# Sixteen like steps per batch: attention's shifted pass, the output projection and the second feed-forward run on into the next iterations, and the stacked q and k are held once

## The reference

```
x = x + 0.5 * ffn(layernorm(x))
x = x + attention(layernorm(x))      # 16 heads of 16, rope on q and k, softmax, output projection W0
x = x + 0.5 * ffn(layernorm(x))
```

## Time and profile before

| | |
|---|---|
| time, median of 3 runs | 1968.64 us (1968.19 to 1973.37) |
| profiled execution | 1970.23 us |
| its span | 1968.4 us |
| TensorE busy | 1812.3 us, 92% |
| VectorE busy | 1270.6 us, 65% |
| ScalarE busy | 986.5 us, 50% |
| GpSimd busy | 503.9 us, 26% |
| granted TensorE clock, mean | 0.973 of full |

### The profile page before, as it was taken

How to read it: one execution, slowest core, us unless ns; L and a number is a source line. 1 busy time by engine, 2 the same in 40 slices (tenths; PEclk the granted TensorE clock), 3 DMA queues, 4 the chain that set the end, 5 groups by cost and what they waited for, 6 DMA issues and landing times.

```text
span 1968.4 us, 26397 instructions
## 1 busy us (share of the span) xinstructions
PE 1812.3 (92%) x9128; PEld 988.0 (50%) x9128; DVE 1270.6 (65%) x2795; ACT 986.5 (50%) x1954; POOL 503.9 (26%) x663
## 2 busy tenths in 40 slices
PE   6598999999999999999999999999999999998885
PEld 5343545454554645455454545545454554545244
DVE  5476776667666766666676676666667666674631
ACT  1245564545555455555545555564555545454541
POOL 1404132141412214141221414122141412213101
PEclk9698999999999999999999999999999999999897
DMA  4513215060320506032050603206050320505000
GB/s 110 91 17 70 39 28 91 12 108 6 64 51 26 94 12 108 4 71 46 27 93 12 108 4 70 47 21 98 12 108 2 67 52 20 100 1 105 4 12 11
DMA packets 96781, 99.40 MB, mean 50 GB/s; under 512 B 19975, under 2 KB 88328, under 8 KB 96520
## 3 DMA queue, kind: packets, MB, share of 16 engines
q1 hardware_dynamic: 93896, 97.19, 26.7%
q10 hardware_dynamic: 2752, 0.54, 0.2%
HBM read 63.54 MB, written 33.55 MB: 49 GB/s over the span
## 4 chain that ended last, share of the span: by engine, by line
PE 61%; DVE 12%; DMA 12%; ACT 4%; SPq 4%; issue 4%; POOL 2%; POOLq 0%; ACTq 0%; DVEq 0%
PE ps L514 10%; PE ps L502 9%; PE ps L581 8%; PE ps L490 8%; DMA scratch<-parts 7%; DVE mx L832 6%; PE ps L560 6%; SPq L475 4%; PE ps L569 4%; DMA out_dram<-x 4%; PE ps L618 3%; PE ps L636 3%; ACT pr L716 2%; PE ps L621 2%; PE ps L681 2%
## 5 line engine op out<-in xcount | busy, mean ns | idle before, releaser
L832 DVE TENSOR_REDUCE mx<-ps 128x1 f32<-128x512 f32 x1024 | 653.5, 682 | 230.6 <-PE ps L490 229.6
L716 ACT ACTIVATE pr<-ps 128x512 f32<-128x512 f32 x1024 | 555.8, 598 | 292.0 <-PE ps L502 291.5
L490 PE MATMUL ps<-stack 96*128 96x512 bf16 x1024 | 326.1, 387 | 27.1 <-DVE mx L832 23.7
L502 PE MATMUL ps<-stack 98*128 98x512 bf16 x1024 | 323.2, 386 | 20.0 <-ACT pr L716 9.5
L514 PE MATMUL ps<-pr,va 128*32 128x512 f32 x2048 | 274.3, 608 | 4.6 <-ACT pr L716 4.6
L502 PEld LDWEIGHTS ps<-stack 98*128 98x128 bf16 x1024 | 77.5, 100 | 273.5 <-ACT pr L716 174.3
L771 ACT ACTIVATE h<-ps,benc 128x512 f32<-128x512 f32 x128 | 88.0, 687 | 216.2 <-PE ps L560 216.2
L490 PEld LDWEIGHTS ps<-stack 96*128 96x128 bf16 x1024 | 97.8, 98 | 187.8 <-DVE mx L832 91.7
L884 DVE SCALAR_TENSOR_TENSOR ps<-ps,wb,h 128x512 f32<-128x512 f32 x128 | 96.7, 755 | 140.7 <-PE ps L569 140.7
L1029 POOL TENSOR_SCALAR rs<-mv 128x4 f32<-128x4 f32 x48 | 11.6, 242 | 608.3 <-DVE mv L852 602.6
L581 PE MATMUL ps<-xh,w_dh 128*128 128x512 f32 x256 | 124.4, 486 | 9.2 <-DVE ps L884 6.7
(11 more groups left out here) (155 smaller groups left out, 2971.0 us busy)
## 6 DMA issues: line engine op xcount, KB each, us to landing
stack<-scratch SPq DMA_DIRECT2D x384, 128.0 KB, 4.5
scratch<-parts SPq DMA_DIRECT2D x64, 384.0 KB, 5.6
xin<-in_L_attn_x_dram SPq DMA_DIRECT2D x16, 512.0 KB, 3.8
out_dram<-x SPq DMA_DIRECT2D x16, 512.0 KB, 6.1
stack<-wu_mT SPq DMA_DIRECT2D x128, 4.0 KB, 1.7
cst<-in_const_dram SPq DMA_DIRECT2D x1, 1024.0 KB
raw<-in_L_ffn_W_dec_dram ACTq DMA_DIRECT2D x1, 512.0 KB, 5.7
pr<-in_L_ffn_W_enc_dram SPq DMA_DIRECT2D x2, 256.0 KB, 7.6
```

The costliest lines, as they stand in the source:

```text
L490: pe.matmul(bank1[:, t % 2, :], stack[b.odd][0][0:KB, hd, 128 * t:128 * t + 128], stack[b.odd][1][0:KB, hd, :], start=True, stop=True).the ...
L502: pe.matmul(bank2[:, a % 2, :], stack[b.odd][1][:, 4 * g + a, 128 * t:128 * t + 128], stack[b.odd][0][:, 4 * g + a, :], start=True, stop=T ...
L716: act.activation(pr[:, n % 2, a, :], bank2[:, a % 2, :], ACT.Exp, scale=SCALE).then_inc(ex_done.sem, 1)
L832: dve.tensor_reduce(mx[:, hd // 4 % 2, e:e + 1], bank1[:, t % 2, :], AX.X, ALU.max).then_inc(mx_done.sem, 1)
```

## The change

`schedule` is written anew. An iteration has 16 steps of two halves (t = 0 to 31). Attention of batch i starts its first pass in iteration i; the second pass stays five steps behind and so reaches to step 4 of iteration i + 1, `pv` to step 5. `nt`, `ot`, `op` and the second feed-forward of a batch stand in the iteration after its first pass from t = 12 on, its `dn` and `up` in the iteration after that (`pp`). `gr` is one step, where it was two parts. Values are held twice, `x1` three times; `xn[2]`, `oT`, `whole` and `squares` are buffers of their own. The stacks of q and k are held once; writing the parts to DRAM (`put`, in `ro3`) and reading them back (`lift`) are separate steps, and `lift` waits until the second pass of the batch before has done half or all of its heads. `nt`, `ot` and `op` use `late` and `early[0]` (`out_bank`), both halves of the first feed-forward's `up` use `early[1]` (`up_bank`), and the waits for banks are changed to suit.

```
+    def attention(s, half):
+        for b, m in ((i, s), (p, s + STEPS)):
+            if not 0 <= b.number < B:
+                continue
+            if LAG <= m < LAG + STEPS: step("s2", b, m - LAG, half)
+        if now:
+            step("s1", i, s, half)
+            if s % 4 == 3 and half: step("ms", i, s // 4)
+        for b, m in ((i, s), (p, s + STEPS)):
+            if not 0 <= b.number < B:
+                continue
+            if LAG < m <= LAG + STEPS and half == (m < LAG + STEPS): step("pv", b, m - LAG - 1)
+    def first_ffn(t):            # batch n
+        t == 0:  tl 0, tl 1, en 0       t == 1: en 1, zs      t == 2: en 2      t == 3: en 3
+        4 <= t < 8: gr t - 4            t == 8: cost, pick    t == 11: dn
+        t == 12: up 0                   t == 13: up 1, st 0   t == 14: st 1, rs
+    def queries(t):              # batch n
+        t == 15: lx 0, lx 1             t == 17: tr 0, tr 1, b0, tl 0, tl 1
+        t == 18: qk 0    19: ro1 0, qk 1    20: ro2 0, ro1 1, va 0    21: va 1    22: ro3 0, ro2 1
+        t == 23: ro3 1, qk 2    24: ro1 2    25: ro2 2, qk 3    26: lift 0, lift 1, ro1 3
+        t == 27: ro3 2, ro2 3   29: ro3 3
+    def second_ffn(t):           # batch p
+        t == 12: nt 0, nt 1    13: nt 2, nt 3    14: ot    15: op 0    16: op 1, st 0
+        t == 17: st 1, rs      18: lx 0, lx 1    20: tr 0, tl 0        21: tr 1, tl 1
+        22 <= t < 26: en t - 22    t == 23: zs   26 <= t < 29: gr t - 26   30: gr 3   31: cost, pick
+    def end_ffn(t):              # batch pp
+        t == 3: dn             t == 9: up 0      t == 10: up 1, store
+    for t in range(2 * STEPS):
+        attention(t // 2, t % 2)
+        if old and t == 0: step("mt", p, 3)
+        if now and t in (8, 16, 24): step("mt", i, t // 8 - 1)
+        if now and t == 10:
+            step("lift", i, 2)
+            step("lift", i, 3)
+        if old: second_ffn(t)
+        if older: end_ffn(t)
+        if new:
+            first_ffn(t)
+            queries(t)
+        if load:                 # batch i + 2
+            t == 14: load    19: st 0    20: st 1, rs    22: lx 0, lx 1    31: tr 0, tr 1
...
-        stack = [[sb(f"stack{o}{a}", [KB + 2, H, S], BF16) for a in range(2)] for o in range(2)]
-        va = sb("va", [128, T, H, 32])
+        stack = [sb(f"stack{a}", [KB + 2, H, S], BF16) for a in range(2)]
+        va = [sb(f"va{o}", [128, T, H, 32]) for o in range(2)]
-        oT = qs
+        oT = sb("oT", [128, C, S])
+        def up_bank(b, f, x):
+            return dense_bank(b, f, x if f else 1)
+        def out_bank(x):
+            return early[0] if x % 2 else late
...
-            def stack_up(b, k):
+            def put(b, k):
                 sp.wait_ge(*lo_done.at(b, k))
-                sp.wait_ge(*ex_done.at(b - 2, H * T - 1))
                 sp.dma_start(scratch[b.odd][k]..., parts[k % 2][:]).then_inc(put_done[k].sem, 16)
+            def lift(b, k):
                 sp.wait_ge(*put_done[k].at(b, 0))
+                sp.wait_ge(*ex_done.at(b - 1, H * T * (k // 2 + 1) // 2 - 1))
                 for j, part in enumerate((Q_PARTS, K_PARTS)[k % 2]):
...
             def natural(b, t):
-                bank = early[t % 2]
+                bank = out_bank(t)
...
             def up(b, f, half):
-                bank = dense_bank(b, f, half)
-                if half == 1:
-                    pe.wait_ge(*(up_done[1].at(b, 0) if f and not final(b) else mid_done[f].at(b, 0)))
+                bank = up_bank(b, f, half)
+                if half == 0:
+                    pe.wait_ge(*mid_done[f].at(b, 0))
+                    if f and b.number + 2 < B:
+                        pe.wait_ge(*mT_done.at(b + 2, 0))
+                else:
+                    pe.wait_ge(*up_done[f].at(b, 0))
...
             def down(b, f):
                 pe.wait_ge(*sel[f].at(b, 3))
+                if f and not final(b):
+                    pe.wait_ge(*mT_done.at(b + 1, 3))
```

More of the change, by code:

```diff
@@ L118, in dense @@
+    def first_ffn(t):
+        if t == 0:
             step("tl", n, 0, 0)
             step("tl", n, 0, 1)
[L120 to L138, removed]
@@ L139, in dense @@
-        if new:
[L140 to L197, removed]
+            step("en", n, 0, 0)
+        if t == 1:
+            step("en", n, 0, 1)
+            step("zs", n, 0)
+            if initial(n): step("w1")
+        if t == 2: step("en", n, 0, 2)
+        if t == 3: step("en", n, 0, 3)
+        if 4 <= t < 8: step("gr", n, 0, t - 4)
+        if t == 8:
+            step("cost", n, 0)
+            step("pick", n, 0)
+            if initial(n): step("w2")
@@ new lines, in second_ffn @@
+    def second_ffn(t):
+        if t == 12:
+            step("nt", p, 0)
+            step("nt", p, 1)
+        if t == 13:
+            step("nt", p, 2)
+            step("nt", p, 3)
+        if t == 14: step("ot", p)
+        if t == 15: step("op", p, 0)
+        if t == 16:
+            step("op", p, 1)
+            step("st", p, 1, 0)
+        if t == 17:
+            step("st", p, 1, 1)
+            step("rs", p, 1)
+        if t == 18:
+            step("lx", p, 1, 0)
+            step("lx", p, 1, 1)
+        if t == 20:
+            step("tr", p, 1, 0)
+            step("tl", p, 1, 0)
+        if t == 21:
+            step("tr", p, 1, 1)
+            step("tl", p, 1, 1)
+        if 22 <= t < 26: step("en", p, 1, t - 22)
+        if t == 23: step("zs", p, 1)
+        if 26 <= t < 29: step("gr", p, 1, t - 26)
+        if t == 30: step("gr", p, 1, 3)
+        if t == 31:
+            step("cost", p, 1)
+            step("pick", p, 1)
@@ L210, in dense @@
-        if at == (23, 1):
-            if now: step("ot", i)
-            if load:
+            if t == 31:
                 step("tr", i + 2, 0, 0)
                 step("tr", i + 2, 0, 1)
[L216 to L223, removed]
@@ L232, in enter, with walk @@
             do[name](first, *args)
-def walk(engine, do):
-    def one(i, number, odd):
-        schedule(do, Batch(number, odd), now=0 <= i < B, old=1 <= i <= B, new=i + 1 < B, load=i + 2 < B)
-    def known(i):
-        one(i, i, i)
-    for i in range(-1, B + 1):
-        known(i)
+def walk(do):
+    for number in range(-1, B + 2):
+        schedule(do, number)
 def macaron(nc, x_in, Wq, bq, Wk, bk, Wv, bv, W0, b0, W_base, b_base, W_enc, b_enc, W_dec, b_dec, W_down, b_down,
@@ L582, in gram @@
                                   start=(c == 0 and w is w_dh and x is xh), stop=False)
+                pe.matmul(bank, gram_w[:, p, :], h[:, p, :], start=False, stop=True).then_inc(gr_full[f].sem, 1)
             def cost(b, f):
```

256 lines of the change are left out of this document (146 added, 110 removed), and 3 rows, old and new, of the table QK.

## The result

The changed kernel takes 2089.4 us (median of 4 runs, 2083.22 to 2091.59), the kernel before 1968.41 beside it (4 runs): a ratio of 1.0606, 95% interval 1.0574 to 1.0637. It is slower, as forecast, but by 121 us and not by 31, and it lies above the range (1928 to 2038). The profiled execution has a span of 2085.6 us.

The account below looks back on a forecast made before the run. TensorE was taken as the bound: 107 us of need and 11.3 of stalls make a 118.3 us period. Fourteen periods plus 344 us for the ends gave 2000 us, range 1928 to 2038.

Parts of the forecast that it names:

- Period: 107 + 11.3 = 118.3 us: Steady period: TensorE's need plus five places' stalls of 12.3 us, less about 1 of first-matmul losses already counted.
- the 107: TensorE's own need per period in us, summed from start-to-start distances of its matmuls in the earlier trace.
- `dn` at t11: First feed-forward's dn waits for GpSimd's copies of the single adapter weights: stall 2.2 us a period.
- Encoder at t0: First feed-forward's encoder waits for ScalarE's six passes and VectorE's low parts after the transposes: stall 2.4 us.
- `qk` at t18: VectorE's load from t12 to t18 holds TensorE 0.75 us at t15 and 2.1 at t18; 3.1 with small ones.
- Encoder at t22: Second feed-forward's encoder waits for GpSimd's low part, behind rotations and deviations: stall 3.6 to 3.8 us.
- `cost` at t8: Short half-step waits for the last decoder reduction, 0.6 us, and 0.2 for the maximum after it.
- The fuller ends win 25 us: First and last iterations win 25 us, less what iterations 1 to 14 lose.
- The spread works: Rival, chance 0.15: GpSimd's and VectorE's chains at t15 to t22 end in time; period 112.4, total 1918 us.
- GpSimd blocked for longer: Rival, chance 0.15: two rotations at their slowest, 2.0 us more a period; period 120.5 to 122, total 2031 to 2052.
- The trade: Rival, chance 0.05: the deeper pipeline only trades the ends against the period; period 116, total 1968 us.
- half-way: Case, chance 0.15: only the t12 to t18 stalls or only the t22 stall gone; period about 114.9, total 1953 us.

Follow-up runs that it names:

- e3: Changed kernel with the third maxima transpose (t24) in bank early[1] instead of late: 2072.79 us, 1.0526 of the kernel before.
- e8: Changed kernel with adapter weights twice, third maxima transpose in another bank, split transposes with early low parts, later second GpSimd rotation: 1939.84 us, ratio to before 0.9858.
- e2: Changed kernel with the adapter's weights held twice, one set for each feed-forward, and pick's wait removed: 2052.16 us, 1.0416 of the kernel before.
- e6: Changed kernel with encoder-input transposes at t29 and t30, their low parts at t30 and the head of t31: 2066.17 us, 1.0492 of the kernel before.
- e12: Kernel e6 with extra matmuls, results overwritten, ahead of the encoder at t22 and of dn at t11: 2014.75 us, 1.0225 of the kernel before.
- e9: Changed kernel with attention's input steps (queries) ahead of the second feed-forward's at t17 and t18: 2088.55 us, 1.0603 of the kernel before.
- e11: Kernel e8 with e9's order, first iteration's lifts at t24, and no wait between the last batch's two up: 1939.22 us, 0.9840 of the kernel before.
- e4: Changed kernel with both transposes of the batch two ahead at t29 instead of t31: 2126.88 us, 1.0794 of the kernel before.
- e5: Changed kernel with extra matmuls, results overwritten, in three gaps (encoder at t22, dn at t11, encoder at t0): 2048.56 us, 1.0404 of the kernel before.

## Why the prediction was wrong

Its direction was right and rests on waits that the runs bear out; the forecast fell 89 us short, 65 of them in fourteen periods (122.94 on the mean, by the stores from 351.4 to 1826.7, against 118.3) and 20 in the ends. The other 4 lie between the median, 2089.4, and the profiled span.

**The step that failed** is "Period: 107 + 11.3 = 118.3 us". It adds the stalls at their lengths to a need of TensorE that is read from the earlier trace rows, at the full granted clock, and has no term for what a stall does to the clock. In the kernel after, the matmuls behind the longest stall (3.1 us) cost 2.4 to 2.6 us more. The profile had a warning: the period before had a clock of 1.00 and no gap over 1.2 us, and the end 0.86. The prediction used the 0.86 for the end alone.

The other half of the miss is the 107. Of the 4.6 us by which the period was missed, the clock has 2.4. The stalls came to 11.1 us for the 11.3 forecast, but not the same ones: the four places that were seen gave 9.2 and the small waits 0.8, and 1.1 came from the copy of the maxima. That leaves 2.3: at the full clock TensorE is busy for 109.3 us a period (e3's period without a fall, and e8's), not 107. Whether these 2.3 us are work that was priced too low or short waits that hide in the overlap of records stays open.

**Places 1 to 5.**
1. `dn` at t11: forecast 2.2, seen 2.1 to 2.2, released by GpSimd's copy; e2 takes it away. Right.
2. Encoder at t0: forecast 2.4, seen 2.5, released by VectorE's low part; e6 takes it away, e12 shows its worth, 2.0. Right.
3. `qk` at t18: forecast 2.1, seen 1.5; the late maximum at t15: forecast 0.75, seen 0.4 (0.17 and 0.21). The place's own totals, 19.6 and gaps of 3 against 21.1, give 1.5. The mechanism is right; that it is worth anything is not shown, since e9 moved it elsewhere for nothing.
4. Encoder at t22: forecast 3.6 to 3.8, seen 3.1, with GpSimd busy all but without a break ahead of it. Right in mechanism, 0.5 too long.
5. `cost` at t8: forecast 0.8, seen 0.2 (for VectorE, at 1079.34); no run tried it.

**Missed:** the encoder's third block at t24 waits for ScalarE's copy of the third transposed maxima, since both use `late`. The prediction called the single bank covered, counting the decoder and the encoder's own readers, and forgot `mt` among its users. 1.1 us in each period (16.1 us in 15).

**The DMAs** at no cost: right. No matmul waits for a lift or a store, and two waits for the maxima's rows cost 1.5 us in the whole run; VectorE's total is 8 us less.

**The ends.** They came to 364 us (2085.6 less 14 x 122.94) where 344 was forecast. The score matmuls of the kernel after, and the clock in three stretches of its head and two of its tail:

```profile
L531 PE MATMUL ps<-stack x1024: 377/379/650, 96.1 to 1995.0; 96*128 96x512 bf16 x171
```

```profile
96.00:126.00 30.00, 25.40 (x87) 14.68 (x88) 19.24 (x42) 4.09 (x7) 2.30 (x8) 0.84 0.12 27
126.00:156.00 30.00, 27.00 (x130) 13.02 (x129) 19.60 (x42) 13.09 (x25) 4.66 (x4) 0.90 0.40 57
156.00:186.50 30.50, 25.95 (x121) 9.71 (x119) 24.16 (x49) 18.25 (x35) 16.70 (x14) 0.89 0.55 103
1946.00:1976.00 30.00, 24.86 (x99) 9.35 (x101) 13.34 (x28) 16.73 (x36) 5.64 (x11) 0.77 0.01 2
2026.00:2085.00 59.00, 36.62 (x130) 26.60 (x130) 9.57 (x29) 9.97 (x21) 6.84 (x15) 0.76 0.03 9
```

By the starts of the score matmuls the parts are: the first 4 us late (96.1 for 92), iteration 0 94 us for 82 (iteration 1 begins at 190.3), and from the start of iteration 15 (1904.3) to the end 181 for 167; the 3 us that were added for first matmuls are in these. The fourteen iterations between took 122.4 each, since iterations 1 and 14 are shorter than the steady ones. Iteration 0 runs at 0.84 to 0.90 of the clock, which again was not priced: up to 186.5 TensorE is busy for 78 us, where 66 of work were counted. The kernel before ran its iteration 0 at 0.86 to 0.94, so this loss is not new, but the shorter iteration was priced without it. The recorded "The fuller ends win 25 us" does not follow from its own sums either: the ends before are 356 us (1968.4 less 14 x 115.15), 12 more than the 344 forecast.

The ends differ by up to 32 us between the kernels of the study (from 582.8 in e11 to 614.5 in e4, as span less twelve periods); what sets them stays open.

**The rivals.** *The spread works* asked for P = 112.4: e8 has this period, but the equal number is chance: the rival kept places 1, 2 and 5 and lost 3 and 4, and e8 keeps 3 and has lost 1, 2 and 4. So the idea can hold a period 2.8 us under the one before; the order as written does not reach it. *GpSimd blocked for longer* fell: the rotations have medians of 1777 and 1272 ns, 0.2 us more for the two than in the earlier trace rows where 2.0 a period was asked, and the wait behind them was shorter than forecast. *The trade* and *half-way* fell with the period.

## What to carry over

Price a wait of TensorE twice: its length, and what the matmuls behind it cost should the granted clock fall. Two or three gaps of 2 to 3 us in a period need not be independent: e3's and e6's edits took away a gap and left the period as it was, since the clock then fell once more, and both were worth 1 to 2 us where it stayed up. So try such edits together, or with filler matmuls that hold the clock, before one is called useless. When a bank is said to be covered, list every writer of it, the small copies too.

## What was not expected of the hardware

A period with three gaps (3.1, 2.5, 2.1 us) had one fall of the clock, behind the longest, in nine of twelve periods. With the 2.1 us gap alone gone (e2) it had one in nine of twelve too, mostly half as long; with the 2.5 us gap gone (e6), or only the 1.1 us one (e3), it mostly had two, and with these the period stayed where it was: medians of 122.8 and 122.9. One period of e3 had no fall at all, with all three gaps. With matmuls in the gaps, the clock stayed at 1.00 and gave 2.4 us a period (e5). Where a fall lands moves with changes elsewhere, by these runs; what decides it they do not show.
